# Graph attention: the records' score words loaded for four groups by one DMA instead of one DMA a group

## The reference

```
h = (x @ W_lin + b_lin).reshape(N, HEADS, EMB)
ee = (edge_attr @ W_edge + b_edge).reshape(-1, HEADS, EMB)
x_i, x_j = h[src], h[dst] + ee
alpha = (x_i * att_i).sum(-1) + (x_j * att_j).sum(-1)
alpha = where(alpha >= 0, alpha, 0.2 * alpha)
e = exp(alpha - segment_max(alpha, src, N)[src])
alpha = e / (segment_sum(e, src, N)[src] + 1e-16)
out = segment_sum(x_j * alpha[:, :, None], src, N).mean(axis=1) + bias
```

## Time and profile before

| what | us |
|---|---|
| median of 3 runs | 16204.83 |
| their range | 16196.27 to 16240.02 |
| the profiled execution's own time | 16222.93 |
| its span, first to last instruction | 16221.2 |
| first to last gather of the attention (line 645 from `h_table`) | 13140.1 to 16109.6 |

### The profile page before, as it was taken

How to read it: one execution, slowest core, us unless ns; L and a number is a source line. 1 busy time by engine, 2 the same in 40 slices (tenths; PEclk the granted TensorE clock), 3 DMA queues, 4 the chain that set the end, 5 groups by cost and what they waited for, 6 DMA issues and landing times.

```text
span 16221.2 us, 180153 instructions
## 1 busy us (share of the span) xinstructions
PE 9592.5 (59%) x40895; PEld 6450.1 (40%) x40896; DVE 7215.4 (44%) x18628; ACT 3844.3 (24%) x8556; POOL 9525.9 (59%) x8465
## 2 busy tenths in 40 slices
PE   0466657766478878845555556655555545555555
PEld 0111122221133333335555554555555545555554
DVE  8876657777000000013333332333333357777776
ACT  0344444442011111112222222222222212222221
POOL 0378878888645434426666664566666645555553
PEclk9999999999688778865555555555555555555555
DMA  9922222222599989992222223222222344444444
GB/s 385 358 15 19 19 15 20 20 20 18 168 342 370 343 306 357 359 113 86 84 86 84 85 84 50 75 84 86 84 86 85 80 95 139 141 141 140 140 139 96
DMA packets 1483063, 2197.01 MB, mean 135 GB/s; under 512 B 882955, under 2 KB 926027, under 8 KB 1454669
## 3 DMA queue, kind: packets, MB, share of 16 engines
q1 hardware_dynamic: 907628, 1490.52, 28.2%
q0 software_dynamic: 453120, 343.50, 12.7%
q10 hardware_dynamic: 121698, 356.43, 6.0%
HBM read 1771.19 MB, written 419.98 MB: 135 GB/s over the span
## 4 chain that ended last, share of the span: by engine, by line
POOL 40%; DMA 22%; issue 21%; PE 8%; DVE 4%; another core or an unknown queue 3%; ACT 1%; POOLq 0%; SPq 0%; DVEq 0%; ACTq 0%
POOL gat L645 18%; POOL adj L613 12%; POOL arena L645 8%; DMA arena<-adj 8%; DMA gat<-q_table,ring_i 6%; DMA arena<-h_table,ring_i 5%; PE bank L1029 5%; DMA adj<-put_n,put_at 2%; POOL rec_src L599 1%; DVE arena L1356 1%; PE same L1161 1%; PE same L1000 1%; DVE arena L1358 1%; PE same L980 0%
## 5 line engine op out<-in xcount | busy, mean ns | idle before, releaser
L645 POOL DMA_INDIRECT gat<-q_table,ring_i x3456 | 3626.6, 1049 | 2405.7 <-DMA gat<-q_table,ring_i 1025.0
L613 POOL DMA_INDIRECT adj<-put_n,put_at x1632 | 2559.9, 1569 | 1265.3 <-DVE put_at L1440 638.1
L1183 PE MATMUL bank<-onehot_t,onehot 128*128 128x64 f32 x6912 | 1585.5, 424 | 2574.9 <-DVE acc L1578 1880.5
L1183 PEld LDWEIGHTS bank<-onehot_t,onehot 128*128 128x128 f32 x6912 | 1506.7, 330 | 2653.8 <-DVE acc L1578 1938.5
L599 POOL DMA_INDIRECT rec_src<-pay,ring_i x1632 | 1606.4, 984 | 1566.9 <-ACTq L743 1093.2
L645 POOL DMA_INDIRECT arena<-h_table,ring_i x1728 | 1729.4, 1001 | 1346.2 <-DMA arena<-h_table,ring_i 760.8
L1088 PE MATMUL same<-onehot 32*128 32x512 f16 x3264 | 1678.6, 615 | 620.0 <-DVE onehot L1411 389.3
L1029 PE MATMUL bank<-arena,hs 128*64 128x512 f32 x5880 | 1596.0, 707 | 508.2 <-DMA arena<-adj 506.9
L1419 DVE TENSOR_SCALAR_CACHE_REDUCE onehot<-same 128x128 bf16<-128x128 f32 (+3 forms) x1632 | 1233.0, 756 | 843.2 <-PE same L1090 675.9
L1173 PE MATMUL bank<-hs,arena 128*128 x6912 | 1564.0, 421 | 29.3 <-ACT arena L867 29.3
L1173 PEld LDWEIGHTS bank<-hs,arena 128*128 128x128 f32 x6912 | 1525.9, 333 | 29.8 <-issue 29.8
(11 more groups left out here) (277 smaller groups left out, 13003.2 us busy)
## 6 DMA issues: line engine op xcount, KB each, us to landing
arena<-adj SPq DMA_DIRECT2D x300, 2560.0 KB
arena<-rec_src SPq DMA_DIRECT2D x432, 552.0 KB
adj<-hs ACTq DMA_DIRECT2D x25, 6656.0 KB, 46.3
rec_src<-pay ACTq DMA_DIRECT2D x1, 119232.0 KB, 332.0
arena<-lo_row SPq DMA_DIRECT2D x432, 256.0 KB
hs<-b_row SPq DMA_DIRECT2D x108, 1024.0 KB
acc<-b_row SPq DMA_DIRECT2D x108, 1024.0 KB
gat<-q_table,ring_i POOLq DMA_INDIRECT x3456
```

What stands on the lines that cost most here:

```text
L613: nc.gpsimd.indirect_dma_start(counts, bass.IndirectOffsetOnAxis(put_at[:, b // 3 % 4, c:c + 1], 0), put_n[:, b // 3 % 4, c:c + 1], None, ...
L645: nc.gpsimd.indirect_dma_start(rows[n][:, u, :], None, table, bass.IndirectOffsetOnAxis(ring_i[:, n, u:u + 1], 0)).then_inc(landed[n], 16)
L1183: last = mm(bank[6 + n % 2][:, u // 2 * D:(u // 2 + 1) * D], onehot[:, n % 2, u, :], msg[n % 2][:, u, :], start=u % 2 == 0, stop=u % 2 == 1)
```

## The change

The ring of eight stays, but it is loaded by halves. In every fourth step (n divisible by 4) SP waits for `t_w` of step n - 1, as before, and loads the ten words of groups n + 4 to n + 7 by one DMA of [128 x 32 x 10] words. In the other three steps the wait for `t_w` and the load are gone. Two semaphores, one for each half, take the place of eight, and DVE's `edge_scores` waits for the half.

```diff
+        rec_flat = arena[:, aend:aend + 8 * U * 10].rearrange("p (t r) -> p t r", r=10)
...
-        t_rec = [sem(f"t_rec{n}") for n in range(8)]
+        t_rec = [sem(f"t_rec{n}") for n in range(2)]
...
             def scores(i, n):
-                if live(i, n + 7):
+                if n % 4 == 0 and live(i, n + 4):
+                    half = (n + 4) % 8 // 4
                     hold(sp, t_w, nth(i, n - 1))
-                    sp.dma_start(rec8[(n + 7) % 8], rec[:, bass.ds(i * (8 * U) + (n + 7) * U, U), 0:10])\
-                        .then_inc(t_rec[(n + 7) % 8], 16)
+                    sp.dma_start(rec_flat[:, half * 4 * U:(half + 1) * 4 * U, :],
+                                 rec[:, bass.ds(i * (8 * U) + (n + 4) * U, 4 * U), 0:10]).then_inc(t_rec[half], 16)
                 if live(i, n + 3):
                     hold(sp, t_m, nth(i, n - 1))
                     hold(sp, t_rel, nth(i, n - 1))
...
-                dve.wait_ge(t_rec[n % 8], i * 16 + (n // 8 * 16 + 16))
+                dve.wait_ge(t_rec[n % 8 // 4], i * 16 + (n // 8 * 16 + 16))
```

## The result

The changed kernel ran at a median of 16238.18 us (16216.84 to 16257.36, 19 runs), the kernel before at 16199.44 us (16174.04 to 16240.02, 19 runs): ratio 1.0022, 95% interval 1.0016 to 1.0029. The change costs 0.22%, some 36 us (38.7 by the two medians), less than the 0.3% that the prediction took for a difference that a measurement tells; with 19 runs a side it is told apart from none.

What follows compares the result with a forecast made beforehand. The prediction took POOL's gather issue and the eighth gather's landing to bound the attention; +13.5 us for low digits and +19 for the long load made +33, so 16,238 us, range 16,140 to 16,330.

Steps and rivals of the forecast that it cites:

- What bounds the stage: Attention: a step lasts as long as eight gathers take to issue, about 9.9 us, then the landing of the eighth.
- Fewer record DMAs: SP's record loads in the attention: 216 become 54 with the same bytes, hidden under SP's wait for ACT; 0 us.
- The rival of the fixed cost: Record loads: a DMA's fixed cost is on the path, so 162 fewer save 324 us, 15,881 us; chance 0.02.
- Low digits in the records' place: Steps 2, 3, 5, 6, 7: low digits move ahead of the eighth gather, +0.10 us a step, 135 steps, +13.5 us.
- the records' leaving: POOL's landing wait: a step without a record load is spared 0.37 to 0.71 us.
- The sign that was asked for: SP's issue of the low digits about half a microsecond behind b_bc, in three steps of four.
- The long load: Step 4: the four-group record load stands partly ahead of the eighth gather; +19 us, bounds 0 to 57.
- one share of 0.71 us: Step 4: of up to three more shares of record engine time ahead of the gather, one was taken, 27 times.
- Step 0: The long load is issued near the landing there and costs the eighth gather nothing.
- The rule on the queues: Engines take queues in turn, at most 64 descriptors a packet; by it the long load's term is 0, sum +14.
- Records late: DVE's edge_scores: records issued two steps, about 27 us, ahead, landing estimated at 2.6 us; 0 us; as rival, chance 0.01.
- The sum: Whole kernel: +13.5 + 19 = +33 us, 16,238 us for the median of runs, within 0.3%.

Runs made afterwards that it cites:

- all_late: The changed kernel with SP waiting for DVE's step to begin (t_b) ahead of both the long record load and the low digits' load; 0.9945 of the kernel before.
- before_late: The kernel before, one group a load, with SP waiting for t_b ahead of both the record load and the low digits' load; 0.9943 of the kernel before.
- wait_kept: The changed kernel with the wait for the last step's weighted rows (t_w) kept ahead of the low digits in every step; 1.0000 of the kernel before.
- lo_late: The changed kernel with SP waiting for t_b ahead of the low digits' load in every step, long load unmoved; 0.9977 of the kernel before.
- two_groups: The changed kernel loading two groups' records every second step in place of four every fourth, with four semaphores; 1.0014 of the kernel before.
- four_dmas: The changed kernel with its long load cut into four DMAs of one group each, issued in a row; 0.9996 of the kernel before.
- long_late: The changed kernel with SP waiting for t_b ahead of the long record load only (steps 0 and 4); 0.9982 of the kernel before.

## Why the prediction came out right, point by point

The time, the sign and the place were right: 16238 us forecast, 16238.18 measured. That the two agree within a microsecond is luck. Two of the terms behind the forecast were not the right size, and their errors cancelled in part; and the forecast was added to a median of three runs, 16204.83, where 19 runs gave 16199.44.

*What bounds the stage.* Right. Stage and wait moved together, within 16 us, in every kernel of the table; both extra waits take 2969.5 to 2867.1 us and 760.8 to 663.8 us, 102.4 and 97.0.

*Fewer record DMAs: 0.* Right within the 32 us that all_late and before_late (0.9945, 0.9943) can tell. The rival of the fixed cost falls with them: the Trainium skill, DMA: Bandwidth & Descriptors, section "Rules for kernel authors", asks to coalesce small transfers, which the prediction's estimate made 324 us. The runs show nothing of that size here, where no one waits for these loads.

*Low digits in the records' place, +13.5 us.* The five steps' waits add up to 6 us less than before (420.4 against 426.4), so the net was near nothing, as the prediction had it, and its sign is not sure (step 1's sum, which nothing here aims at, ranges over 14 us between these kernels). Both halves were priced too high. wait_kept has the records out of these steps and half as many of the low digits ahead as the change: 46.5 us less than before, 0.36 us a step, and 40.5 us less than the change, 0.31 us a step. By lo_late, which has none of the low digits ahead, the two are 0.50 and 0.45 us. So the records' leaving was worth some 0.36 to 0.50 us, the lower part of the 0.37 to 0.71 that was given, and the low digits cost 0.31 to 0.45, not the 0.67 to 0.87 of their engine time. The place was right and the distance was not: the low digits run close behind the scores' load, whose last piece ends about 1 us after POOL's last gather, so they moved 1.65 us forward (2.54 to 0.89), not 4. The sign that was asked for, SP's row half a microsecond behind the scores' load, did not come (4.58 us), but that row does not tell the time of the issue. Why the low digits start 0.55 us later with the wait kept, and what keeps SP in between, is not settled.

*The long load, +19 us of 0 to 57.* The mechanism and the step were right, the size was not. Step 4's wait grew from 2.95 to 4.93 us in the turn shown and by 2.00 us on average, 26 x 2.00 = 52 us. The prediction took one share of 0.71 us because records and gathers had been seen side by side; it should have stayed near the upper bound. In place of 1,024 runs 3,675 started ahead of the gather's last piece; at the prediction's 11.1 ns a run the 2,651 more take 1.84 us on 16 engines. The same working gives 0.71 us for two_groups and 0.32 for four_dmas, where step 4's wait grew by 0.78 and 0.37. long_late takes the cost back. Step 0, where the load comes with the landing, was put at nothing; its wait grew by 0.29 us, 7.5 us in all.

*The rule on the queues.* The trace has 1,549 runs, some 97 an engine, go by from 14635.2 to 14635.9 us without one piece of the gather, and the wait grew by 2.00 us. The Trainium skill, DMA: Bandwidth & Descriptors, section "Queues, rings and completion order", has a DMA engine pass from one queue with work to the next after a packet of at most 64 descriptors. By that rule, the prediction said, this term would be 0; the trace does not agree, and the measurement decides; whether the gather's own descriptors were there in time to be taken is open. In four_dmas the gather got past the records earlier, but SP issued those four over 3.24 us, so that run does not tell shorter DMAs from later ones.

*Records late.* Right, no one waits for them. From issue to landing the long load took a median of 5.4 us (4.7 to 6.7), twice the 2.6 of the estimate but a fifth of the two steps that it has:

```profile
DMA to landing us min/median/max: 4.7/5.4/6.7
```

*The sum.* Step 4 +52, the five steps -6, step 0 +7.5 and step 1, which the prediction left out, -9: +44 on the wait, 39 on the stage and 36 by the ratio, against +33.

## What to carry to other kernels

Ask of a background load when it runs, before asking how many DMAs it takes: here a load for which nobody waits cost time with the part of it that ran ahead of one that everybody waits for. Making it longer and rarer turned several small collisions into one large one, and the gap that it left in the queue was taken by what SP issued next. One wait on a semaphore that is counted right after the critical landing was worth 0.55%, with long loads or short ones.

## What the runs showed of the hardware that was not expected

One DMA of 4,096 runs of 40 bytes held up a gather of another queue for some 2.4 us in a step (5.04 us in the change, 2.67 with the same load behind the landing in long_late), one of 1,024 runs for about 0.5 (3.04 before, 2.57 in before_late). And SP's row of a DMA can come later than its packets: the row of the low digits stands 0.96 to 0.99 us ahead of their first piece in most steps of the kernel before, and in four steps of the change up to 0.43 us behind it (medians).
